# First batch of two latent attention layers: the products for the row maxima, two query tiles at a time in the two halves of TensorE's rows

## The reference, cut to what matters

```python
q_hk = (hidden_q @ Wq.T).reshape(b, s, H, K)
q_big = jnp.einsum('bshk,hkq->bshq', q_hk, w_kc_q)
q_r = jnp.einsum('bshq,hqr->bhsr', q_big, W_qr)
k_r = jnp.einsum('bld,hdr->bhlr', kv_rope, W_kr)
scores = jnp.einsum('bhsr,bhlr->bhsl', q_r, k_r)
attn = jax.nn.softmax(scores, axis=-1)
ctx_c = jnp.einsum('bhsl,bld->bhsd', attn, kv_rope)
```

## Time and profile before

| | us |
|---|---|
| median of 3 runs | 2282.21 |
| lowest and highest run | 2281.89, 2282.95 |
| span of the profiled execution, first to last instruction | 2276.6 |
| stretch of layer 2 (from the stage's first make to the first L1397) | 409.90 to 430.42 |
| stretch of layer 4 | 1735.17 to 1755.51 |
| busy share: TensorE, weight loads, VectorE, ScalarE, GpSimd | 94%, 67%, 68%, 46%, 65% |

### The profile page before, as it was taken

One profiled execution on the slowest core, in us unless ns is written; L12 is line 12 of the kernel. 1 busy time (PEld: TensorE's weight loads), 2 busy tenths in 40 slices (PEclk: granted clock), 3 DMA queues, 4 the chain that ended last, 5 costly groups with the idle time before them and its releaser, 6 DMA issues.

```text
span 2276.6 us, 30620 instructions
## 1 busy us (share of the span) xinstructions
PE 2145.4 (94%) x11236; PEld 1519.8 (67%) x11236; DVE 1540.0 (68%) x2492; ACT 1036.5 (46%) x1533; POOL 1482.0 (65%) x933
## 2 busy tenths in 40 slices
PE   7797999999999997898999999979998999999988
PEld 5585777766666664565666666578896666666588
DVE  6766863588888856666787888653335787888653
ACT  4452333555555445212555545434335555545443
POOL 0355763488888873465888888724443888888744
PEclk9798999999999998898999999989999999999989
DMA  3126875211121104001111111025531111111022
GB/s 93 44 74 190 254 239 148 74 42 41 41 61 42 28 29 131 24 1 42 41 42 61 41 41 43 6 84 150 145 85 55 41 42 60 41 42 43 6 65 82
DMA packets 60640, 160.14 MB, mean 70 GB/s; under 512 B 9669, under 2 KB 19669, under 8 KB 60108
## 3 DMA queue, kind: packets, MB, share of 16 engines
q1 hardware_dynamic: 60108, 157.86, 23.2%
q10 hardware_dynamic: 384, 0.33, 0.1%
HBM read 143.18 MB, written 14.98 MB: 69 GB/s over the span
## 4 chain that ended last, share of the span: by engine, by line
PE 83%; DVE 6%; ACT 3%; issue 2%; POOL 2%; DMA 2%; SPq 1%; ACTq 0%; PEldq 0%; DVEq 0%; POOLq 0%; PEld 0%
PE psum L922 21%; PE psum L1426 19%; PE psum L1416 10%; PE psum L1397 10%; PE psum L1418 10%; PE psum L1580 2%; PE psum L1443 2%; PE psum L1537 2%; PE psum L1303 1%; PE psum L1181 1%; POOL CL L1871 1%; DMA WqrT<-in_a_WrT 1%; PE psum L1201 1%; PE psum L1277 1%; ACT E L1849 0%
## 5 line engine op out<-in xcount | busy, mean ns | idle before, releaser
L1849 ACT ACTIVATE E<-psum 125x896 f32<-125x896 f32 x576 | 528.1, 920 | 574.4 <-PE psum L1418 546.9
L2417 DVE TENSOR_REDUCE mx<-psum 128x1 f32<-128x500 f32 x945 | 611.8, 675 | 166.5 <-PE psum L1397 164.5
L2151 POOL TENSOR_TENSOR SA<-SA,E 125x896 f32<-125x896 f32 x282 | 597.4, 2118 | 22.1
L1426 PE MATMUL psum<-E,V 125*64 125x448 f32 x2304 | 472.0, 544 | 0.0
L1416 PE MATMUL psum<-Q,K 128*125 128x448 f32 x1152 | 332.1, 369 | 2.3 <-ACT E L1849 2.3
L1397 PE MATMUL psum<-K,Q 128*128 128x500 f32 x945 | 328.8, 402 | 2.6 <-ACT Q L1836 2.2
L1418 PE MATMUL psum<-Q,K 128*125 128x448 f32 x1152 | 330.3, 368 | 0.0
L1426 PEld LDWEIGHTS psum<-E,V 125*64 125x64 f32 x2304 | 171.6, 136 | 213.9 <-issue 202.5
L2151 POOL TENSOR_TENSOR SA<-SA,SB 125x896 f32<-125x896 f32 x93 | 194.2, 2088 | 148.5 <-DVE SB L2440 148.5
L1397 PEld LDWEIGHTS psum<-K,Q 128*128 128x128 f32 x945 | 174.5, 188 | 134.3 <-issue 34.7
L1416 PEld LDWEIGHTS psum<-Q,K 128*125 128x125 f32 x1152 | 213.2, 187 | 37.0 <-ACT E L1849 6.9
(11 more groups left out here) (299 smaller groups left out, 3591.5 us busy)
## 6 DMA issues: line engine op xcount, KB each, us to landing
K<-kt_scratch SPq DMA_DIRECT2D x48, 750.0 KB, 4.8
K<-kt_scratch SPq DMA_DIRECT2D x48, 375.0 KB, 6.0
EW<-in_f_w SPq DMA_DIRECT2D x64, 256.0 KB, 8.3
kt_scratch<-kt SPq DMA_DIRECT2D x16, 750.0 KB, 7.7
WS<-in_f_w SPq DMA_DIRECT2D x31, 384.0 KB, 4.6
GB<-gates_scratch SPq DMA_DIRECT2D x36, 224.0 KB, 3.9
slot_of_t<-slots_scratch SPq DMA_DIRECT2D x64, 112.0 KB, 4.8
WoT<-in_a_WoT SPq DMA_DIRECT2D x24, 256.0 KB, 4.2
```

Of the source, the lines that this page charges most:

```text
L1426: i = e.matmul(psum[c * DC:(c + 1) * DC, 4 + b % 2, 0:HT], V[0:LP, b, k * DC:(k + 1) * DC], E[g[n, b, k] % NE][0:LP, half[c]], start=k == ...
L1849: e.activation(E[m % NE][0:LP, :].rearrange("p (c q) -> p c q", c=2), psum[0:LP, pair:pair + 2, 0:HT], ACT.Exp).then_inc(exp_set.sem, 1)
L2151: e.tensor_tensor(SA[b % 2][0:LP, :], a[0:LP, :], x[0:LP, :], ALU.add).then_inc(sum_set.sem, 1)
L2417: e.tensor_reduce(mx[:, b % 2, j * 3 + c:j * 3 + c + 1], psum[:, bank, 0:CW], AX.X, ALU.max).then_inc(small_free.sem, 1)
```

## The change

In layers 2 and 4 (`n != 2`) the tiles j = 0 to 5 of the first batch go in pairs (0,1), (2,3), (4,5). A pair is issued where its odd tile stood; at the place of its even tile only the waits of j = 0 are left. The even tile uses rows 0 to 63 of `K1t` and `Q1n`, the odd tile rows 64 to 127 of `K2t` and `Q1n`; both hold high parts. The three products of the even tile and the three of the odd one alternate. A pair waits until the odd tile of the pair before was reduced, so that all six banks are free. At tile 0 there is a new wait for `K2t` of the first batch. Tile 6 stays as it was. The maxima of tiles 0 to 5 are those of the high parts' products alone; the low keys' share is left out there.

```diff
+    def pe_tile_pair(e, n, b, j):
+
+        if j >= 2:
+            e.wait_ge(*small_free.at(n, "max_tile", b, j - 1))
+        for c in range(3):
+            for odd, keys in enumerate((K1t[b % 3], K2t[b % 2])):
+                rows = slice(odd * DC, (odd + 1) * DC)
+                i = e.matmul(psum[:, 3 * odd + c, 0:CW], Q1n[b % 3][rows, tok(j + odd)], keys[rows, c * CW:(c + 1) * CW], start=True, stop=True)
+                if c == 2:
+                    i.then_inc(small_made.sem, 1)
+
     def pe_core(e, n, tasks):
@@
                 if j == 0:
                     e.wait_ge(*k1_in.at(n, b))
                     e.wait_ge(*q1_set.at(n, b, 3))
+                    if n != 2:
+                        e.wait_ge(*k2_in.at(n, b))
+                if n != 2 and j < NT - 1:
+                    if j % 2 == 1:
+                        pe_tile_pair(e, n, b, j - 1)
+                    continue
                 if j >= 2:
                     e.wait_ge(*small_free.at(n, kind, b, j - 2))
```

## The result

The changed kernel takes 2287.28 us (median of 18 runs), the kernel before 2279.98 us (18 runs): ratio 1.0031, 95% interval 1.0022 to 1.0039, which is 7.1 us slower (5.0 to 8.9). The span of the profiled execution went from 2276.6 to 2284.5 us.

What follows compares the result with a forecast made beforehand. TensorE was taken to bound the kernel, products busy 94% of the span. Wait, hand-over and entering pairs add 5.25 us (2.2 and 3.05 in layers 2 and 4), the clock 1.35: 2282.2 + 6.6 = 2288.8 us, range +3.4 to +10.5.

Steps and rivals of the forecast that it cites:

- 5.6 us kept around the span: Whole kernel: the 5.6 us between the profiled span of 2276.6 and the runs' median of 2282.21 were to stay.
- The wait for `K2t`: At tile 0's place, ahead of make 2: TensorE waits for `K2t`, landing 4.1 and 4.8 us after issue; make 2 stands behind.
- The hand-over: Between pairs: all six banks must be free, so VectorE waits 0.04 + 1.10 us for the next pair's products.
- Changing to half rows: On entering each pair: switching from full rows costs 0.10 us, bounds 0 and 0.2; leaving hides under a stall.
- The clock: At tile 6 and make 7: TensorE's thin place likely drops the clock to half; 1.35 us, bounds 0 and 2.7.
- The small terms: Layers 2 and 4: release 0.04 us, tile 6 0.80 with make 7 1.40, landings 4.1 and 4.8, gaps 0.04 + 1.10.
- No overlap: In the pairs: halves don't work at once, 2.5 us more, 2291.3 us; chance 0.22 together with loads in line.
- Loads in line behind their own half's product: In the pairs: a half's next load waits for its product, 0.4 us a pair, 2.3 in all; shares 0.22.
- Hand-over only, without a fall of the clock: Layers 2 and 4: no loss of clock and no drain, 4.65 us slower, 2286.9 us; chance 0.23.
- TensorE's own work decides: At the end of make 7: each pair saves its 0.67, 4.0 us in all, 2278.2 us; chance 0.06.
- Absorbed later: Behind the start of the scores: the delay vanishes, leaving 2282.2 us; chance 0.04.

Runs made afterwards that it cites:

- e10: Changed kernel with six more products (make 7's, result unused) between pair (4,5) and tile 6; ratio to the kernel before 1.0008.
- e9: Kernel before with only the wait for `K2t` added at tile 0, ahead of make 2; ratio to the kernel before 1.0009.
- e1: Changed kernel with its wait for `K2t` moved from tile 0's place to the first pair, behind make 2; ratio to the kernel before 1.0024.
- e2: Changed kernel with pairs on all 128 rows of `K1t`, no half rows and no wait for `K2t`; ratio to the kernel before 1.0015.
- e7: Kernel of e6 with make 7 moved ahead of tile 6; ratio to the kernel before 0.9969.
- e8: Changed kernel with `K2t`'s wait at the first pair, `bd`'s wait at its first use and make 7 ahead of tile 6; ratio to the kernel before 0.9986.
- e4: Kernel before, tile by tile, with tiles 0 to 5 on half rows and the wait for `K2t` at tile 1; ratio to the kernel before 1.0003.
- e3: Changed kernel with a pair's loops exchanged: three products of the even tile, then three of the odd; ratio to the kernel before 1.0025.
- e6: Kernel before with VectorE's wait for the mask `bd` moved from its program's head to the mask's first use; ratio to the kernel before 0.9955.

## Why the prediction was right

The prediction was 2288.8 us, 6.6 above the 2282.2 of the runs then shown; measured are 7.1 above before and 2287.28, inside the range. Slower by over 0.2% had 0.73, and it came. That 6.6 lies so near 7.1 is partly luck: the traces put the loss at 8.2, and the clock's share of it is 1.7 larger than the forecast has it. The stretches grew by 3.9 and 4.6 us, 8.5 in sum; less the clock's 3.1 (e10) that leaves 5.4 for the wait and the hand-over, where 5.25 were forecast. The 5.6 us kept around the span are another matter: the profiled execution after the change took 2286.23 us with a span of 2284.5, so 1.7 lie around it, and the rest of the 5.6 is the difference between one execution and others. By its steps:

**The wait for `K2t`** was right in place and size. It landed 4.0 and 4.5 us after its issue (4.1 and 4.8 taken). The release took 0.25 us instead of the 0.04 seen between engines; all makes stood behind it. With the mask to open the chain in its stead, it is worth 1.2 to 1.6 us in all (e9, e1).

**The hand-over** was right and is the largest part: of the 8.5 us by which the stretches grew, the clock has 3.1 and the wait 1.2 to 1.6, and about 4 are left. The gaps of VectorE are 1.03 and 1.04 (1.14 predicted). e2 shows it without half rows and without the wait. It is dear beside a kernel whose VectorE idles only 0.6 us because the mask comes late; e7 and e8 show it to cost next to nothing where VectorE waits for every tile anyway.

**Changing to half rows** was taken at 0.10 on entering each pair, and that was wrong both ways. The first pair starts 0.10 late (413.76, the product before it at 413.43, where 0.23 apart is usual), and its second products another 0.10 late: 0.2, as in e4 on each side. Pairs (2,3) and (4,5) pay nothing: behind a stall the third product of the even tile starts 0.55 us after its first (418.24 and 418.79), and on full rows behind a stall before the change it was 0.56 (418.03 and 418.60). So 0.2 a layer stands against 0.3 forecast. By the Trainium skill, TensorEngine Tiling (Array Packing), Key Properties, a change of mode drains the engine; e4's rows agree, at 0.2 us each.

**The clock** is the term that was mis-sized: 1.35 taken, 2.7 as the bound. Measured by e10 it is 1.5 a layer, 3.1, above the bound. The step that failed took the fall to come 1.2 and 0.5 us after the restart, as before. It came within 0.1 us of tile 6's start in both layers (0.07 ahead of it in layer 2), so that nearly all of tile 6 and make 7 ran at 1.2 GHz. That the fall depends on chance too, e3 shows with one layer of each kind. The small terms missed in both directions and nearly cancel: the release behind the DMA was 0.21 too low, tile 6 with make 7 was 0.16 too low (2.20 taken, 2.36 in e10 at 2.4 GHz), the landings were 0.1 and 0.3 and each gap 0.1 too high.

**The rivals.** No overlap: fell, a pair takes 0.95 us for six products, and in either order (e3); the even tile's third product came 0.55 us after its first, where 0.85 was the sign of no overlap. The kernel before could have told: its 32 half-row products L1341 were read as 49 ns apart in the mean, but in the trace they start in twos, 7 ns apart, each two some 92 ns behind the one before. Loads in line behind their own half's product: fell with it. The second load of each half lies at 418.34 to 418.53, while both first products (418.24 to 418.73) still run, and the products of a half follow each other as closely as on full rows. By the Trainium skill, TensorE: Matmul & The Clock Gate, Part 3, loads overlap a product only on other row groups; these rows don't agree. Hand-over only, without a fall of the clock (4.65 us): fell, the clock fell in both layers and cost 3.1, and the interval of the timed loss begins at 5.0. TensorE's own work decides: fell, its stall before tile 6 alone is 1.8 us. Absorbed later: fell, the ways differ by 8.2 and the span by 7.9.

## What to carry to other kernels

Before work is made quicker by pairing it, look at what the pair needs at once: here all six banks, which turned a double buffer into a single one, and the 0.4 us of TensorE that each pair saved was paid with 1.03 us of VectorE standing still between pairs. A stall costs twice if it lets TensorE's clock fall for the work behind it; work of no use in the stall was cheaper than the stall (e10). And a chain that starts at a wait which the waiting instruction doesn't need is the first thing to mend: moving one line gave 8.5 us by the traces and 10 us in the timed runs (e6).

## What the runs showed of the hardware

- Products on rows 0 to 63 and on rows 64 to 127 run at the same time even when issued as three and three: six of 500 columns in 0.95 us (e3), in either order. Half-row products of 56 columns start in twos, 7 ns apart (L1341, kernel before).
- Going from full rows to half rows and back costs 0.2 us each where TensorE doesn't come from a stall (e4: 1.60 against 1.40 for a make, 0.88 against 0.67 for a tile), and nothing on entering behind a stall (0.55 against 0.56 us, changed kernel and before).
- TensorE's first product behind a DMA's landing starts 0.25 us after it (changed kernel and e3, both layers), against 0.04 behind another engine.
- The same stall was followed by 2.4 GHz in one layer and by 1.2 GHz in another of one execution (e3); six of eight such stalls were followed by the fall within 0.8 us of the restart, so a stall makes it likely and not certain.
